# The causal mask of the scores: a bfloat16 matmul, or an addition in PSUM by VectorE

## The reference

```python
q, k, v = (to_heads(q), to_heads(k), to_heads(v))
q, k = _rope(q), _rope(k)
att = jnp.einsum('bhqd,bhkd->bhqk', q, k) * scale
causal = jnp.tril(jnp.ones((t, t), dtype=bool))
att = jnp.where(causal, att, -jnp.inf)
att = jax.nn.softmax(att, axis=-1)
y = jnp.einsum('bhqk,bhkd->bhqd', att, v)
```

## Time and profile before

| | us |
|---|---|
| median of 3 runs | 4748.85 (4747.68 to 4749.20) |
| the profiled execution, its own time | 4746.46 |
| its span, from first to last instruction | 4744.3 |
| TensorE matmuls busy | 4298.7 (91%) |
| TensorE weight loads busy | 2166.4 (46%) |
| VectorE busy | 2877.1 (61%) |
| ScalarE busy | 2251.6 (47%) |
| GpSimd busy | 1470.2 (31%) |

### The profile page before, as it was taken

One profiled execution on the slowest core, in us unless ns is written; L12 is line 12 of the kernel. 1 busy time (PEld: TensorE's weight loads), 2 busy tenths in 40 slices (PEclk: granted clock), 3 DMA queues, 4 the chain that ended last, 5 costly groups with the idle time before them and its releaser, 6 DMA issues.

```text
span 4744.3 us, 73590 instructions
## 1 busy us (share of the span) xinstructions
PE 4298.7 (91%) x18016; PEld 2166.4 (46%) x18016; DVE 2877.1 (61%) x5831; ACT 2251.6 (47%) x4226; POOL 1470.2 (31%) x983
## 2 busy tenths in 40 slices
PE   3999999976989999887999999878899999859998
PEld 1444444443444444353444444354444444347776
DVE  2556667555656666475557666475556766465565
ACT  0237777722257777522267767422267777411111
POOL 1532223222522223313422223304322223304554
PEclk8989999997989999998999999989899999979999
DMA  4331222222432122123322122123422222219998
GB/s 143 130 117 50 60 60 68 65 78 77 138 90 66 50 63 72 50 96 99 127 77 66 54 68 62 60 91 102 138 53 61 61 65 55 92 57 251 258 257 196
DMA packets 320327, 453.53 MB, mean 96 GB/s; under 512 B 143012, under 2 KB 150308, under 8 KB 316964
## 3 DMA queue, kind: packets, MB, share of 16 engines
q1 hardware_dynamic: 298408, 390.40, 27.1%
q0 software_dynamic: 21504, 58.40, 5.3%
HBM read 285.91 MB, written 168.56 MB: 96 GB/s over the span
## 4 chain that ended last, share of the span: by engine, by line
PE 65%; issue 19%; POOL 5%; ACT 4%; DVE 3%; DMA 2%; SPq 1%; POOLq 1%; ACTq 0%; DVEq 0%
PE PS L1105 23%; PE PS L1062 14%; PE PS L1084 11%; PE PS L1207 5%; PE PS L1218 3%; PE PS L1133 3%; POOL qs L787 2%; POOL t L784 2%; ACT Pt L929 2%; PE PS L1087 1%; PE PS L1146 1%; PE PS L1178 1%; PE PS L1193 1%; POOLq L534 1%; PE PS L1139 1%
## 5 line engine op out<-in xcount | busy, mean ns | idle before, releaser
L929 ACT ACTIVATE Pt<-PS 128x512 f32<-128x512 f32 (+3 forms) x2560 | 1232.1, 534 | 784.9 <-PE PS L1087 408.0
L1344 DVE TENSOR_REDUCE part<-PS 128x1 f32<-128x512 f32 x1536 | 1019.4, 686 | 711.7 <-PE PS L1062 711.3
L1105 PE MATMUL PS<-Pt,V 128*64 128x512 f32 (+3 forms) x5120 | 1276.1, 560 | 0.0
L1062 PE MATMUL PS<-QK 96*128 96x512 f32 (+3 forms) x2560 | 873.7, 424 | 57.6 <-DVE part L1344 28.3
L813 POOL TENSOR_TENSOR ot<-ot,od 32x512 f32<-32x512 f32 x256 | 326.5, 1275 | 1771.2 <-ACT od L915 1771.2
L1084 PE MATMUL PS<-QK 97*128 97x512 f32 (+3 forms) x2560 | 825.4, 390 | 16.2 <-ACT Pt L929 8.1
L1062 PEld LDWEIGHTS PS<-QK 96*128 96x128 f32 x2560 | 394.9, 192 | 891.5 <-DVE part L1340 408.0
L1340 DVE CUSTOM_DVE_ANT_0 PS<-PS,consts 128x128 f32<-128x128 f32 (+3 forms) x1024 | 500.6, 495 | 150.5 <-PE PS L1062 149.5
L1084 PEld LDWEIGHTS PS<-QK 97*128 97x128 f32 x2560 | 480.9, 193 | 153.2 <-ACT Pt L929 52.1
L1049 PE MATMUL PS<-hT,W 128*128 128x512 f32 x1024 | 452.9, 595 | 3.5 <-ACT hT L878 3.5
L1105 PEld LDWEIGHTS PS<-Pt,V 128*64 128x64 f32 x5120 | 255.9, 135 | 313.1 <-issue 246.6
(11 more groups left out here) (151 smaller groups left out, 4127.9 us busy)
## 6 DMA issues: line engine op xcount, KB each, us to landing
QK<-qkd SPq DMA_DIRECT2D x720, 128.0 KB, 3.0
qkd<-st SPq DMA_DIRECT2D x64, 1024.0 KB, 4.5
Wg<-wgu SPq DMA_DIRECT2D x48, 768.0 KB
Wd<-wdn SPq DMA_DIRECT2D x48, 384.0 KB
xin<-x SPq DMA_DIRECT2D x16, 1024.0 KB, 5.4
vd<-vst SPq DMA_DIRECT2D x16, 1024.0 KB, 6.3
table<-modd SPq DMA_DIRECT2D x64, 256.0 KB, 3.9
xc<-x SPq DMA_DIRECT2D x16, 1024.0 KB, 7.5
```

Of the source, the lines that this page charges most:

```text
L929: nc.scalar.activation(Pt[:, t % NPT, first:CH], S2[t % NS2][:, first:CH], ACT.Exp, scale=SCALE).then_inc(exp_done, 1)
L1062: mm(s1[:, 0:w], QK[0:3 * HD, hh % 2, 0, qb * P:(qb + 1) * P], QK[0:3 * HD, hh % 2, 1, c * CH:c * CH + w], start=True, stop=True).then_inc ...
L1105: last = mm(O[j % 2][2 * i * HD:2 * (i + 1) * HD, first:CH], values_and_ones(g, kb + i, hh % GH), Pt[:, (2 * n + i) % NPT, first:CH], star ...
L1344: v.reduce_max(part[:, qb, cc:cc + 1], s1[:, 0:w], AX.X).then_inc(s1_dve, 1)
```

## The change

The matmul on line 1087 goes, with `idbf` and `mtbf`. A new table `causal` holds the same mask in fp32. A new step `("mask", hh, u)` stands in the list directly behind the score step of the 8 diagonal units of each head. In it VectorE waits for each of the two tiles (`s2_ready`), adds the mask in PSUM in place and raises `masked_done`. ScalarE waits for `masked_done` where it waited for `s2_ready`; on the other 12 units it waits as before. `N_MASK` counts the masks of one sequence, 256.

```diff
@@ stream()
         out.append(("score", *divmod(n, NU)))
+        if ONDIAG[n % NU]:
+            out.append(("mask", *divmod(n, NU)))
         if n >= 2:
             out.append(("value", *divmod(n - 2, NU)))
@@ adaln_block(), buffers
-        idbf = place("idbf", [P, P], BF16)
-        mtbf = place("mtbf", [P, 2 * P], BF16)
+        causal = place("causal", [P, 2 * P], F32)
@@ ScalarE, step "score"
-                            act.wait_ge(s2_ready, ONE + NPT_B * b + t + 1)
+                            if ONDIAG[u]:
+                                act.wait_ge(masked_done, ONE + N_MASK * b + 2 * (sum(ONDIAG) * hh + sum(ONDIAG[:u])) + i + 1)
+                            else:
+                                act.wait_ge(s2_ready, ONE + NPT_B * b + t + 1)
@@ TensorE, step "score"
-                            last = mm(S2[t % NS2][:, first:CH], QK[0:3 * HD + 1, hh % 2, 1, k * P:(k + 1) * P],
-                                      QK[0:3 * HD + 1, hh % 2, 0, j * CH + first:(j + 1) * CH], start=True, stop=masked == 0)
-                            if masked:
-                                last = mm(S2[t % NS2][:, first:first + masked], idbf[:, :], mtbf[:, 2 * P - masked:2 * P], start=False, stop=True)
-                            last.then_inc(s2_ready, 1)
+                            mm(S2[t % NS2][:, first:CH], QK[0:3 * HD + 1, hh % 2, 1, k * P:(k + 1) * P],
+                               QK[0:3 * HD + 1, hh % 2, 0, j * CH + first:(j + 1) * CH], start=True, stop=True).then_inc(s2_ready, 1)
@@ VectorE
+                    elif kind == "mask":
+                        _, hh, u = step
+                        j, kb = UNITS[u]
+                        for i in range(2):
+                            t = 2 * (NU * hh + u) + i
+                            first, masked = extent(j, kb + i)
+                            corner = S2[t % NS2][:, first:first + masked]
+                            dve.wait_ge(s2_ready, ONE + NPT_B * b + t + 1)
+                            v.tensor_tensor(corner, corner, causal[:, 2 * P - masked:2 * P], ALU.add).then_inc(masked_done, 1)
```

More of the change, by code:

```diff
@@ L94 @@
 ENDS = [max(u for u in range(NU) if UNITS[u][0] == j) for j in range(NCH)]
+ONDIAG = [kb >= TPC * j for j, kb in UNITS]
 NPT = 8
@@ L177 @@
 NV, NPT_B = NU * H, 2 * NU * H
+N_MASK = 2 * sum(ONDIAG) * H
 STEPS = front() + stream()
@@ L448, in adaln_block @@
         s2_ready = sem("s2_ready")
+        masked_done = sem("masked_done")
         exp_done = sem("exp_done")
@@ L1079, in _ @@
                             t, k = 2 * (NU * hh + u) + i, kb + i
-                            first, masked = extent(j, k)
+                            first, _ = extent(j, k)
                             if t >= NS2:
                                 pe.wait_ge(exp_done, ONE + NPT_B * b + t - NS2 + 1)
-                            last = mm(S2[t % NS2][:, first:CH], QK[0:3 * HD + 1, hh % 2, 1, k * P:(k + 1) * P],
-                                      QK[0:3 * HD + 1, hh % 2, 0, j * CH + first:(j + 1) * CH], start=True, stop=masked == 0)
-                            if masked:
-                                last = mm(S2[t % NS2][:, first:first + masked], idbf[:, :], mtbf[:, 2 * P - masked:2 * P], start=False, stop=True)
-                            last.then_inc(s2_ready, 1)
+                            mm(S2[t % NS2][:, first:CH], QK[0:3 * HD + 1, hh % 2, 1, k * P:(k + 1) * P],
+                               QK[0:3 * HD + 1, hh % 2, 0, j * CH + first:(j + 1) * CH], start=True, stop=True).then_inc(s2_ready, 1)
                     elif kind == "value":
@@ L1247, in _ @@
             v.tensor_copy(onesbf[:, :], kset[:, K_ONE - KEPT:K_ONE - KEPT + P])
-            v.tensor_copy(idbf[:, :], K[:, K_ID:K_ID + P])
-            v.tensor_copy(mtbf[:, :], kset[:, K_MT - KEPT:K_MT - KEPT + 2 * P])
+            v.tensor_copy(causal[:, :], kset[:, K_MT - KEPT:K_MT - KEPT + 2 * P])
             v.tensor_copy(tcol[:, :], K[:, K_T4:K_T4 + TPC])
```

## The result

The changed kernel takes **4810.95 us** (median of 4 runs, 4810.20 to 4817.50), against 4748.80 for the kernel before on the same chip: 62 us more, ratio 1.0134, 95% interval 1.0117 to 1.0152. I had said 4767, with a range that ended at 4805. The sign and the mechanism were right, the size was a third of what came.

What follows compares the result with a forecast made beforehand. TensorE sets the pace in the stream, with ScalarE as tight from unit 1 to 5. Boundaries, pairs 10 and 11 and first units sum to +4.6 a sequence, +18 for four: 4746.5 + 18 + 2.4 = 4767 us, range 4732 to 4805.

Steps and rivals of the forecast that it cites:

- the mechanism: Diagonal units: exponentials wait for VectorE's masks, queued behind row maxima and some reciprocals, so TensorE waits for ScalarE at score banks.
- ordinary boundary: Passage between heads, from unit 18 into the next head, without reciprocals before masks: 0.08 us slower, 12 per sequence, +1.0.
- the start of the copies: ScalarE's copies behind unit 1's exponentials: start 8.56 us after unit 18's start, in place of 8.35.
- Ordinary pairs 10 and 11: Diagonal units 10 and 11 of heads without reciprocals there: four masks' saving of 0.36 us stays, -4.3 us per sequence.
- The price of a mask: One mask matmul costs TensorE 0.095 us; removing them saves 1.6 us a head, 103 us for 64 heads.
- just free in time: Units 10 and 11: the score bank is free when TensorE wants it, so the 0.36 us saving stays.
- Where reciprocals stand: Heads 3, 7, 11, 15, reciprocals ahead of masks: boundary 2.2 us slower, units 10 and 11 +0.55; +6.6 and +1.7 per sequence.
- TensorE alone decides: Rival for the whole stream: each removed mask's 0.095 us is gained, 4748.9 - 103 = 4646 us; chance 0.08.
- wholly on TensorE: Where the removed mask matmuls' time lies: 1.6 us a head, 103 us for 64 heads.
- ScalarE's row: Gapless exponentials and copies from unit 1 to unit 5: moves 0.2 us later at ordinary boundaries, 2.1 more with reciprocals.
- The hand-over is dearer: Rival: mask plus hand-over to ScalarE takes 0.3 us more than 0.35, at 60 boundaries and pairs; 4803 us, chance 0.16.
- the pipeline that must be empty before the next operation: Rule on VectorE: if it held between a unit's two masks, the second comes 0.08 us later, 5 us more, 4772.

Runs made afterwards that it cites:

- unit 1 alone: VectorE adds only unit 1's masks, behind both row maxima and any reciprocal; TensorE keeps the other 14 mask matmuls of a head; +69.3 us against the kernel before.
- the other place: Changed kernel with VectorE multiplying the corner of Pt after the exponential, in place of adding before it; 57.5 us less than the kernel before.
- four banks: Four score banks and two for row maxima, not three and three, negated maximum earlier: changed kernel +34.9 us, kernel before +84.5, against the three-bank kernel before.
- split kernel: Changed kernel, but VectorE masks only units 18, 19, 0, 10, 11, between the maxima; TensorE masks 1, 4, 5; negated maximum earlier; 4686.45 us, ratio 0.9864.
- reciprocals moved: Split kernel with chunk 2's four reciprocals, and the product behind them, three units later in heads 3, 7, 11 and 15; -56.2 us against the kernel before.

## Why the prediction was wrong in size and right in kind

*The mechanism held.* The operation takes 294 ns (0.29 predicted). The Trainium skill (VectorE: DVE Perf Modes, The TRN2 errata) has (N+151)/0.96 ns for an fp32 addition of two inputs; by it I estimate 291 ns at 128 columns and 424 at 256, and the trace agrees, with 294 and 420. The masks stand behind the maxima and reciprocals; ScalarE's copies move; TensorE waits at units 2, 4 and 5. Experiments with unit 1 alone, with the other place and with four banks each show one link of it.

*The ordinary boundary: +0.08 predicted, +0.50 measured*, 48 times, 20 of the 42 us that were missing in the streams (+18.4 us predicted, +60.4 measured). The step that failed is the start of the copies, which I put at 8.56 and which came at 8.91 in the boundary that I had worked out. Of the 0.35: unit 1 starts 0.17 later than I had it (6.08 for 5.91), since unit 19 keeps only 0.06 of its saving of 0.2; the masks of unit 1 reach ScalarE 0.05 later (VectorE's mask ends at 596.92 by its 0.29, the exponential starts at 597.03, where I took 0.06); and 0.13 is a slip of mine, for I had the exponentials end at 8.66 and the copies start at 8.56, while in the trace they follow 0.58 after the start of the exponentials. A second part of the step failed too: I had the row move by 0.2 and the boundary by 0.08, since by my steps unit 6 started exactly as before, and I gave no reason for that. All kernels with three banks but one show that the boundary takes over the move of the copies in full.

*Ordinary pairs 10 and 11: -0.36 predicted, -0.17 measured*, 9 us. The price of a mask was right, -0.20 at unit 10. But unit 11 saved nothing (0.00) in the changed kernel and 0.19 in the kernels where the exponentials are early. Its tiles are narrow, so its second tile comes early to the bank of the first exponential of unit 10: it starts 0.05 after that exponential has ended, where 1.15 lay between them in the kernel before. I had called it "just free in time"; it is not.

*Where reciprocals stand: boundary 2.2 predicted, 2.5 measured in the three streams after the first; pair +0.55 predicted, +0.66 measured*, 5 us together. Here nearly every step was as worked out. Head 3, VectorE:

```profile
463.67 0.95 DVE L1377 RECIPROCAL den<-den 128x128 f32<-128x128 f32 x1
464.53 0.47 DVE L1371 TENSOR_TENSOR PS<-PS,causal 128x128 f32<-128x128 f32 x2
```

and TensorE, with the waits at the second tiles of units 19, 1 and 2 (predicted 0.74 at unit 19):

```profile
465.57 0.33 PE L1091 MATMUL PS<-QK 97*128 97x128 f32 x1 [0.69 <-ACT Pt L936]
...
470.46 0.33 PE L1091 MATMUL PS<-QK 97*128 97x128 f32 x1 [0.39 <-ACT Pt L936]
...
472.81 0.51 PE L1091 MATMUL PS<-QK 97*128 97x512 f32 x1 [0.57 <-ACT Pt L936]
```

*Not foreseen: the clock*, 3 us, in the first stream alone (next but one section). The last 5 of the 42 us are spread over the first and last heads and the units between, below 0.1 each; I have no single cause for them.

*The rivals.* "TensorE alone decides" (4646) is refuted by the changed kernel, but it marks what the freed time is worth with no wait behind it: 71 us, not the 103 that I had called "wholly on TensorE". That was a wrong step too, and it cancelled out, since I let ScalarE's row eat all 12 savings of a boundary. "The hand-over is dearer" (4803, "decides from about 0.1 of extra delay") was nearest, and in part by its mechanism: from a mask's start to its exponential's start 0.40 to 0.44 pass for my 0.35 (596.63 to 597.03, 590.30 to 590.74), though that is only 0.05 of the 0.35 by which the copies were late. I gave it 0.16, although a tenth of a us in the chain goes straight into 60 boundaries and 60 pairs, and the chain has several links that no row of the kernel before could show. The range should have reached some 20 us further up.

*The rules.* The Trainium skill (Perfetto Trace Analysis, Identifying the Most-Contended Engine) has one optimize the busiest engine first. Here that engine was relieved and the kernel got slower; the split kernel relieves it by 10 masks of 16 and is faster. The rule picked the right engine and says nothing on which of its instructions are free. The other rule was the pipeline that must be empty before the next operation. Two masks of 294 ns take 0.53 together at 590.30 and 0.49 at 596.63, so the second starts 0.20 to 0.24 after the first, before that has ended, as the row maxima do. The prediction saw a contradiction in such rows. The Trainium skill (VectorE: DVE Perf Modes, The DRAIN you can't avoid) goes on, though, that a next operation that is not held starts earlier; I had quoted half of the rule, and the overlap alone doesn't speak against it.

## What to carry to other kernels

Before work moves from a busy engine to an idle one, look where its result is needed next and what stands in front of it in the idle engine's queue: here one mask in eight, the pair whose consumer stands ahead of a gapless row on a third engine, cost as much as all of them. Move the work only where its consumer has slack, leave it where the busy engine waits anyway (there it is free), and count the buffers between producer and consumer: one bank more for the scores turned the same change from +62 to -50 us, each against a kernel with the same banks. And when a chain of hand-overs decides, widen the range by some hundredths of a microsecond for each link, times the number of repetitions.

## What the hardware showed that I had not expected

**Half the clock after a few waits, sometimes.** In the first stream of the changed kernel, after the waits of the boundary behind head 3, TensorE's granted clock fell from 1.00 to a mean of 0.58 in the 8 us that follow, that is to the lower of its two levels, 1.2 for 2.4 GHz, for most of them:

```profile
465.00:472.00 7.00, 6.00 (x24) 2.61 (x24) 6.95 (x15) 2.53 (x6) 0.00 (x0) 1.00 0.52 124
472.00:480.00 8.00, 7.43 (x22) 3.16 (x22) 4.05 (x16) 6.24 (x12) 3.75 (x3) 0.58 0.30 88
480.00:490.00 10.00, 10.00 (x44) 4.27 (x40) 8.43 (x23) 8.17 (x16) 2.51 (x2) 1.00 0.31 82
```

The four value matmuls at 473.25 take 1.98 us where others take 1.08. Units 2, 3 and 4 of the head that follows lose 1.72, 1.16 and 0.78 where the same units lose 0.83, 0.08 and 0.46 in the other three streams, which have the same boundary and kept a clock of 1.00. In the same stream it came once more, behind head 11 (0.76 over the 7 us from 807), and the kernels with the masks ahead of the maxima and with four banks have single places like it (0.81, and 0.76 and 0.80). What sets these apart I did not find.

```profile
473.25 1.98 PE L1109 MATMUL PS<-Pt,V 128*64 128x512 f32 x4
...
602.15 1.08 PE L1109 MATMUL PS<-Pt,V 128*64 128x512 f32 x4
```

**The rest of the program isn't constant.** The span less the four stretches of stream is 2322.8 us in the kernel before, and between 2314.6 (split) and 2331.4 (reciprocals moved) in the others with three banks, though little in it was edited: the first and last units of the streams, 235 to 241 us of it in these kernels. The routing of the last sequence shows one place, in windows set at the same work (split, then reciprocals moved): the clock, 1.00 or 0.91.

```profile
4100.00:4140.00 40.00, 35.79 (x190) 22.43 (x188) 33.77 (x70) 10.35 (x16) 1.02 (x1) 1.00 0.15 56
```

```profile
4103.00:4143.00 40.00, 35.84 (x189) 22.78 (x189) 31.42 (x59) 9.71 (x15) 1.02 (x1) 0.91 0.15 56
```

The kernel before has 0.91 at this place. What decides it I did not test. For the reader it means, as my estimate from these spans, that a total is good for some 8 us either way when two edits of the stream are compared, and that the stretch that was edited should be measured by itself.

**An operation in SBUF that GpSimd held up.** With the masks behind the exponential, the fp32 operation on 128 columns of `Pt` has a mean of 367 ns, against 294 in PSUM. It isn't a slower operation: half of them took 284 ns or less (288 in PSUM), and the mean comes from 77 of the 1024 masks that took 0.5 to 1.4 us. All 77 ran while GpSimd was at an operation of its own in SBUF, 72 of them beside its addition of line 819. VectorE, then GpSimd:

```profile
396.61 1.61 DVE L1371 TENSOR_TENSOR Pt<-Pt,causal 128x128 f32<-128x128 f32 x2
```

```profile
396.60 1.27 POOL L819 TENSOR_TENSOR den<-den,od 32x512 f32<-32x512 f32 x1
```

The first of the two masks takes 1.41 us and ends 0.15 after GpSimd's addition. Another 82 masks met GpSimd and stayed below 0.5 us. No run changed GpSimd's work, so that it holds VectorE up is read from where the long ones stand, not tested.
